# An attention and feed-forward kernel on one core: the mixed values are copied out of PSUM in two parts instead of one

## The reference

```python
xn = _layernorm(x, axis=-1)
# attention
q = jnp.einsum('bsd,hde->bhse', x, wq) + bq        # k, v alike
scores = jax.nn.softmax(jnp.einsum('bhse,bhte->bhst', q, k) * scale, axis=-1)
att = jnp.einsum('bhst,bhte->bhse', scores, v)
att = att.transpose(0, 2, 1, 3).reshape(b, s, h * e)
att @ wo.T + bo
# feed-forward, on the same xn
xr = mu_r * x + (1.0 - mu_r) * x_prev              # xk alike
r = sigmoid(xr @ W_r); k_act = square(relu(xk @ W_k)); out = r * (k_act @ W_v)
# result
x + attention(xn) + feed_forward(xn)
```

## Time and profile before

| what | value |
| --- | --- |
| median of 3 runs | 470.46 us (470.16 to 470.57) |
| the profiled execution's own time | 470.89 us |
| its span, first to last instruction | 468.7 us |
| mean granted TensorE clock | 0.978 |
| PE, DVE, ACT, POOL busy | 449.2, 400.7, 390.2, 366.5 us |

### The profile page before, as it was taken

How to read it: one execution, slowest core, us unless ns; L and a number is a source line. 1 busy time by engine, 2 the same in 40 slices (tenths; PEclk the granted TensorE clock), 3 DMA queues, 4 the chain that set the end, 5 groups by cost and what they waited for, 6 DMA issues and landing times.

```text
span 468.7 us, 15677 instructions
## 1 busy us (share of the span) xinstructions
PE 449.2 (96%) x5254; PEld 271.7 (58%) x5254; DVE 400.7 (85%) x824; ACT 390.2 (83%) x865; POOL 366.5 (78%) x674
## 2 busy tenths in 40 slices
PE   5689999999989999999999999999999999999996
PEld 4245656556656556666665656566656666665554
DVE  7579989989988999899999999899998999989831
ACT  2038989989878998989899989889898989899884
POOL 6668888888878988788888888888888888887321
PEclk9569999999999999999999999999999999999999
DMA  4534355454445545344554544355544444455100
GB/s 137 154 115 142 100 140 162 127 154 133 111 132 148 157 127 153 108 131 132 146 158 129 155 139 126 105 144 155 158 134 138 137 124 122 140 151 146 50 15 24
DMA packets 86061, 60.43 MB, mean 129 GB/s; under 512 B 6224, under 2 KB 73808, under 8 KB 86032
## 3 DMA queue, kind: packets, MB, share of 16 engines
q1 hardware_dynamic: 86032, 60.06, 44.9%
HBM read 29.89 MB, written 29.36 MB: 126 GB/s over the span
## 4 chain that ended last, share of the span: by engine, by line
PE 87%; DMA 3%; issue 3%; ACT 2%; DVE 2%; SPq 1%; ACTq 0%; DVEq 0%; POOL 0%
PE bank_val L625 26%; PE bank_exp L701 19%; PE bank_max L711 10%; PE misc L730 4%; PE misc L752 4%; PE misc L640 4%; PE misc L659 3%; PE misc L741 3%; PE misc L793 3%; PE misc L786 3%; PE misc L667 2%; PE misc L767 2%; ACT probs L454 1%; PE misc L762 1%; DMA ops<-spill 1%
## 5 line engine op out<-in xcount | busy, mean ns | idle before, releaser
L551 DVE TENSOR_REDUCE neg_max<-bank_max 128x2 f32<-128x512 f32 x512 | 327.5, 683 | 40.5 <-PE bank_max L711 35.0
L454 ACT ACTIVATE probs<-bank_exp 128x512 f32<-128x512 f32 x504 | 272.8, 596 | 27.7 <-PE bank_exp L701 27.6
L711 PE MATMUL bank_max<-ops 48*128 48x256 bf16 x1024 | 163.7, 277 | 0.0
L701 PE MATMUL bank_exp<-ops 51*128 51x256 bf16 x1008 | 158.1, 272 | 5.5 <-issue 3.2
L625 PE MATMUL bank_val<-probs,val 128*25 128x256 f32 x2048 | 136.3, 384 | 0.8 <-ACT probs L454 0.8
L701 PEld LDWEIGHTS bank_exp<-ops 51*128 51x128 bf16 x1008 | 72.6, 94 | 72.5 <-issue 48.0
L625 PEld LDWEIGHTS bank_val<-probs,val 128*25 128x25 f32 x2048 | 50.4, 103 | 51.8 <-issue 26.3
L711 PEld LDWEIGHTS bank_max<-ops 48*128 48x128 bf16 x1024 | 74.9, 95 | 5.3
L356 POOL TENSOR_SCALAR xn<-x_in,moments,rstd 128x128 f32<-128x128 f32 x62 | 49.2, 801 | 0.0
L395 POOL TENSOR_TENSOR mixed_x<-mixed_x,xn_t 128x512 f32<-128x512 f32 x32 | 40.7, 1272 | 2.5
L370 POOL TENSOR_TENSOR qk_l<-qk_rest,qk_m 128x512 bf16<-128x512 f32 x31 | 36.0, 1162 | 2.5
(11 more groups left out here) (76 smaller groups left out, 619.7 us busy)
## 6 DMA issues: line engine op xcount, KB each, us to landing
ops<-spill SPq DMA_DIRECT2D x126, 192.0 KB, 3.4
spill<-qk_h SPq DMA_DIRECT2D x64, 192.0 KB, 3.4
spill<-qk_m SPq DMA_DIRECT2D x64, 128.0 KB, 1.9
x_in<-x SPq DMA_DIRECT2D x32, 128.0 KB, 2.2
spill<-qk_l SPq DMA_DIRECT2D x32, 128.0 KB, 1.8
y_out<-y SPq DMA_DIRECT2D x32, 128.0 KB, 1.9
ops<-shift SPq DMA_DIRECT2D x128, 6.0 KB
w<-weights SPq DMA_DIRECT2D x1, 448.0 KB, 3.0
```

The lines of the kernel that those rows point to most:

```text
L454: nc.scalar.activation(probs[g % 2][:, u % G, :, :], exp_bank(u, live)[:, :, :], ACT.Exp, scale=SCALE).then_inc(exp_done[u], 1)
L551: nc.vector.tensor_reduce(out=neg_max[hf][:, :, r, pr], in_=bank_max[MAX_BANK[v]][:, :, :], axis=AX_X, op=ALU.max, negate=True).then_inc(m ...
L701: exp_mm = nc.tensor.matmul(exp_bank(u, live)[:, i, :], ops[p][rows, hf, 1, pr, i * P:(i + 1) * P], ops[p][rows, hf, 0, pr, :], start=True ...
L711: max_mm = nc.tensor.matmul(bank_max[MAX_BANK[v]][:, i, :], of[rows, max_hf, 0, max_pr, i * P:(i + 1) * P], of[rows, max_hf, 1, max_pr, :] ...
```

## The change

The single copy of 128x512 is split by halves of `bank_val`. The first half, which is final after value call 1, is copied behind exponential 11 of the same step, after two waits: for `mix_psum[1]` of this batch, and for `tokens_psum` of the batch before, because its transposes read `mixed`. The second half stays at the old place behind exponential 1 of the next step, now 128x256. Where no step t+1 follows, the whole bank is copied as before. Since both halves lie in one PSUM bank, PE now waits for the new semaphore `mixed_first` ahead of value call 2 (behind unit 13), so that it doesn't write the bank while ACT reads it.

```diff
                     if u == 1 and live(-1):
                         act.wait_ge(mix_psum[NG - 1], n(-1))
-                        nc.scalar.copy(mixed[:, :, :], bank_val[:, :, :]).then_inc(mixed_done, 1)
+                        rows = slice(1, 2) if live(0) else slice(0, 2)
+                        nc.scalar.copy(mixed[:, rows, :], bank_val[:, rows, :]).then_inc(mixed_done, 1)
...
+                    if u == 11 and live(0) and live(1):
+
+                        act.wait_ge(mix_psum[1], n(0))
+                        after(act, tokens_psum, n(-1))
+                        nc.scalar.copy(mixed[:, 0, :], bank_val[:, 0, :]).then_inc(mixed_first, 1)
                     if u == 11 and live(1) and live(0):
                         act.wait_ge(hidden_psum, n(1))
                         move_values(1 - p, far, n(1))
...
                     if u == (13 if live(1) else 15) and live(0):
+                        if live(1):
+
+                            pe.wait_ge(mixed_first, n(0))
                         mix_values(2, n(0), n(-1), p)
```

More of the change, by code:

```diff
@@ L177, in split_attention_ffn_kernel @@
         mix_psum = [sem(f"mix_psum{g}") for g in range(NG)]
-        mixed_done, tokens_psum = sem("mixed_done"), sem("tokens_psum")
+        mixed_first, mixed_done, tokens_psum = sem("mixed_first"), sem("mixed_done"), sem("tokens_psum")
         inv_done, att_done = sem("inv_done"), sem("att_done")
```

## The result

| | before | changed |
| --- | --- | --- |
| median, 22 runs each, interleaved | 470.53 us | 468.32 us |
| ratio, 95% interval | | 0.9955 (0.9941 to 0.9968) |
| profiled execution: time, span | 470.89, 468.7 us | 468.32, 466.2 us |

The change makes the kernel 0.45% faster (0.32% to 0.59%). That is 2.2 us by the medians and 2.5 by the two spans; the forecast was 3.0. One of the 22 runs of the changed kernel, at 472.90 us, was in a slower state and is left out of the ratio.

A forecast was written before the change was run, and what follows sets the result against it. PE was taken to bound the kernel, filling the whole 13.39 us step. Closing the gap at unit 5 gains 3.0 us and the added copy and wait cost 0: 467.9 us profiled, 467.5 as median, range 466.4 to 469.2.

The forecast's parts named there:

- The place and its size: PE's unit 5 starts 0.12 us late, waiting for exponential 3, in 25 steps; closing this gains 3.0 us.
- The half copy: Behind exponential 1 on ACT: slot falls from 0.48 to 0.27 us, so exponentials 2 and 3 come 0.21 us earlier.
- Rival 1: At unit 5 only part of the gap closes, half being left: 469.0 us, chance 0.10.
- The added copy at 0: Copy of 128x256 behind exponential 11 falls in ACT's idle time before the values' copy, costing 0.
- Rival 2: ACT sets the pace or the gain is taken back elsewhere: about no change, 469.6 to 471.4 us, chance 0.08.
- PE's wait at 0: PE's new wait ahead of value call 2: copy 0.70 us early, at most 0.3 us in all, taken as 0.
- ACT's busy time: ACT's busy time over the kernel rises by 5.3 us, its slots by 1.9 us.
- Rival 3: Longer program makes PE load code at the loop's five jumps: slower, 472.1 us, chance 0.05.
- rival 4: More than forecast: PE's first-pass gaps, 2.7 us, may shift when code moves; 466.8 or 466.6 us, chance 0.05.
- The total: Whole kernel: 3.0 us gained, 0 to 0.3 given back, median 467.5 us; full gain's chance 0.72.
- The move from the profile to the median: Profiled execution of 470.89 us lies 0.43 above the runs' median of 470.46, so 467.9 becomes 467.5.

The follow-up runs named there:

- halve_only: Kernel before with only the copy behind exponential 1 halved, first half not copied after the first step, no new PE wait: 468.59 us, ratio 0.9968.
- add_copy: Kernel before with its full copy kept, plus a first-half copy behind exponential 11 into a spare tile and PE's wait: 470.55 us, ratio 1.0004.
- quarter_first: Changed kernel with only a quarter of the bank copied early and three quarters behind exponential 1: 469.88 us in one time, ordinary steps 13.28 us.
- late_copy: Changed kernel with the early copy one exponential later, behind exponential 12: 490.8 us, ratio 1.0417 to the kernel before.
- busy_start: Changed kernel with filler matmuls on the identity while PE waits in the steps before step 0: 478.84 us, ratio 1.018.
- before_2: Kernel before, unchanged, profiled once more: span 470.1 us, ordinary step 13.39 us.
- after_2: Changed kernel, unaltered, profiled once more: span 467.7 us, ordinary step 13.26 us.

## Why the prediction was right, point by point

*The place and its size.* The gap was 0.12 us in 25 steps. It closed in all 25, and the ordinary step shortened by 0.13, 25 x 0.13 = 3.2 us; the profiles' means over steps 1 to 31 are 3.1 apart. halve_only and add_copy show that the whole effect on the step sits in the copy behind exponential 1.

*The half copy* was costed at a slot of 0.27 us from the gate and took 0.26. quarter_first, in a single profile, confirms the end of exponential 3 as the criterion, down to 0.02 us a step. Rival 1, part of the gap, didn't come.

*The added copy at 0.* Right. It began 0.12 us before exponential 11 ended (0.1 assumed) and the values' copy kept its place. Rival 2 falls with add_copy, where an ACT that sets the pace would have cost 8 us and the step stayed at 13.39. The Trainium skill's page "ScalarE: Activation LUTs", section "What ACT_TABLE_LOAD costs", charges a fixed part for each instruction, 186 ns where scale and bias are immediate, and 0.833 ns per element. The slope is what this case shows: 571, 463, 357 and 272 ns for 512, 384, 256 and 128 columns, (571 - 357) / 256 = 0.836 ns a column. The durations are lower than the 612 and 399 ns for 512 and 256 columns, an estimate from the Trainium skill's two figures; here the fixed part comes to 143 ns (571 - 512 x 0.836). A fixed part there is, and it was paid: the two halves take 357 + 378 = 735 ns against 571, but in idle time.

*PE's wait at 0.* Right, but its slack was misread. The prediction took 0.12 us off the start of value call 2 "once 0.12 is gone" and left the copy where it was; both keep their distance from the unit 5 before them (value call 2 starts 7.18 us behind it before and 7.17 after, exponential 11 ends 6.09 and 6.08 behind it), so the slack is 231.47 - 230.64 = 0.83 us, not 0.70. late_copy shows what the wait costs past that.

*ACT's busy time* was to rise by 5.3 us and rose by 3.9, since the page counts overlapping time once; the step view's 0.13 x 31 = 4.0 agrees. That figure bore on nothing.

*Rival 3, code at the loop's jumps.* The steps behind the five jumps take 13.67 to 13.94 us, as before (13.75 to 13.87). At the jump itself PE has no such gap, as forecast. But in the changed kernel one stands behind value call 0 of step 12, the first step behind the second jump:

```profile
199.08 0.27 PE L707 MATMUL bank_exp<-ops 51*128 51x256 bf16 x1 [0.19 <-issue]
```

It isn't the longer program's doing: the kernel before has it at the same place in both its repeats (0.27 and 0.29 us), and no profile of either kernel has it behind all five jumps. So rival 3 didn't come, though a single profile of the kernel before couldn't show this. The gaps of the first pass moved about from profile to profile (2.1 to 4.6 us in all for one and the same kernel), so rival 4's idea that a shift of code sets them isn't needed.

*The total.* 468.32 us against 467.5, inside the range of 466.4 to 469.2. The ratio's upper end of gain is 0.59%, 2.8 us, a little short of 3.0; the two repeats put it at 0.5% (0.2% to 0.8%). The place and the mechanism were right; what the medians show less of is the size, 2.2 us for 3.0. The move from the profile to the median isn't to blame: it took 0.43 us off, and the median of the kernel before over 22 runs, 470.53, is within 0.07 of the 470.46 used. The medians of the three sessions with both kernels differ by 2.2, 3.3 and 2.5 us, and start and gaps alone scatter by 1.1 and 2.5 us between executions. So the forecast's 3.0 lies just outside the interval of the first comparison and inside those of the two repeats. Whether the unprofiled runs gain 2.2 or 3.0 us these intervals don't settle, and where a missing part would go isn't shown.

## What to carry to other kernels

When the busiest engine is shown full, compare starts of the same pair of matmuls where nothing can hold them and where something might: here 0.23 against 0.35 us gave 3.0 us, where the steps show 3.2 and the medians 2.2. Splitting work on another engine pays if the late piece gets off the path and the early piece falls where that engine waits anyway. In add_copy the fixed cost of the second piece was then too small to measure, and in late_copy a place one exponential later cost ten times the gain. Past the point where the waiting engine is no longer held, moving more work brings next to nothing: the second quarter of the bank brought 0.02 us a step.

## What the runs showed that was not expected

- TensorE stayed at its lower clock for 16 us in which PE was shown busy without a break (busy_start, 20 to 36 us), with fp32 and bf16 matmuls mixed. A busy share of 1 in the profile didn't mean the upper clock there.
- The recorded clock can miss the slow phase. halve_only shows 1.00 for 36 to 40 us, the first row below, while a value call takes 1.58 us in place of 1.06, the second, from its timeline of PE:

```profile
36.00:40.00 4.00, 4.00 (x41) 1.99 (x40) 2.33 (x5) 2.45 (x5) 2.70 (x7) 1.00 0.34 101
...
37.08 1.58 PE L626 MATMUL bank_val<-probs,val 128*25 128x256 f32 x16
```

  before_2 and after_2 read 1.00 from 24 to 34 us as well, with score matmuls of 0.39 to 0.42 us in place of 0.28. In this kernel the matmuls' durations are the surer sign of the clock.

- The gaps of PE without a cause differ by over 2 us between profiles of the same kernel. Most stand where code runs for the first time, and without the loop there are 10 of them, 5.5 us, up to the end; a few of 0.16 to 0.45 us stand in later rounds of the loop. That they are code loading is plausible and wasn't shown.
